# Local transformer: ScalarE writes the masks into PSUM and copies both halves of the turned probabilities

## The reference

```python
q, k, v = heads(shift(x) @ Wqkv)        # 16 heads of 64
q, k = l2norm(q) * q_scale, l2norm(k) * k_scale
q, k = rotate(q, scale), rotate(k, 1 / scale)
# windows of 32 queries; keys of the same window and the one before
sim = einsum('bhwie,bhwje->bhwij', q, look_back(k)) * 8
mask = (i < j) | (i > j + 32) | (j == -1)
attn = softmax(where(mask, -max, sim))
x = einsum('bhwij,bhwje->bhwie', attn, look_back(v)) @ Wo + x
x = (a * gelu(gate)) @ W2 + b2 + x      # a, gate = layernorm(shift(x)) @ W1 + b1
```

## Time and profile before

| | |
|---|---|
| median of the runs | 2441.62 us |
| the profiled execution | 2439.11 us, span 2437.3 us |
| TensorE matmul busy | 2257.1 us (93%) |
| TensorE weight load busy | 1530.4 us (63%) |
| VectorE busy | 1855.8 us (76%) |
| ScalarE busy | 1298.4 us (53%) |
| GpSimd busy | 1154.0 us (47%) |

### The profile page before, as it was taken

One profiled execution on the slowest core, in us unless ns is written; L12 is line 12 of the kernel. 1 busy time (PEld: TensorE's weight loads), 2 busy tenths in 40 slices (PEclk: granted clock), 3 DMA queues, 4 the chain that ended last, 5 costly groups with the idle time before them and its releaser, 6 DMA issues.

```text
span 2437.3 us, 83769 instructions
## 1 busy us (share of the span) xinstructions
PE 2257.1 (93%) x36453; PEld 1530.4 (63%) x36453; DVE 1855.8 (76%) x4174; ACT 1298.4 (53%) x2414; POOL 1154.0 (47%) x855
## 2 busy tenths in 40 slices
PE   8999899889999999999999999999999999979985
PEld 4567554446667666666667676666766676655564
DVE  5742588779988889798888889897888888756612
ACT  3524154355666666656566666656566666525332
POOL 1037300046666556565656556565656556410064
PEclk8989899899999999999999999999999999999898
DMA  9012200000111211121101211021111111130012
GB/s 297 31 31 41 59 1 1 5 27 20 41 29 37 68 33 31 35 68 37 42 20 37 69 45 33 20 68 37 42 26 31 33 46 33 34 109 2 21 37 77
DMA packets 63736, 106.92 MB, mean 44 GB/s; under 512 B 11700, under 2 KB 48831, under 8 KB 56844
## 3 DMA queue, kind: packets, MB, share of 16 engines
q1 hardware_dynamic: 57626, 93.00, 13.5%
q0 software_dynamic: 4736, 8.29, 1.7%
q10 hardware_dynamic: 1010, 0.29, 0.1%
HBM read 42.55 MB, written 13.24 MB: 23 GB/s over the span
## 4 chain that ended last, share of the span: by engine, by line
PE 62%; POOL 12%; DVE 11%; issue 10%; ACT 3%; DMA 2%; SPq 0%; POOLq 0%; ACTq 0%; DVEq 0%
PE ps L2213 10%; PE ps L2316 6%; PE ps L2295 5%; POOL mem L3007 5%; PE ps L2257 4%; PE ps L2234 4%; PE ps L2222 4%; PE ps L2272 3%; POOL mem L3020 3%; PE ps L2382 3%; PE ps L2368 2%; PE ps L2359 2%; PE ps L1196 2%; POOL mem L3014 2%; PE ps L1682 2%
## 5 line engine op out<-in xcount | busy, mean ns | idle before, releaser
L3007 POOL TENSOR_TENSOR mem<-mem 128x512 f32<-128x512 f32 x384 | 571.6, 1495 | 557.2 <-DVE mem L2524 554.0
L2213 PE MATMUL ps<-mem 128*128 128x512 f32 x768 | 380.8, 608 | 8.6 <-ACT mem L2811 3.4
L2839 ACT ACTIVATE mem<-ps 128x512 f32<-128x512 f32 x384 | 221.5, 603 | 155.7 <-PE ps L2234 155.1
L2818 ACT ACTIVATE mem<-ps 128x512 f32<-128x512 f32 x384 | 220.6, 597 | 144.1 <-PE ps L2213 107.3
L2519 DVE TENSOR_TENSOR mem<-ps,mem 128x512 f32<-128x512 f32 x384 | 258.5, 673 | 13.0 <-ACT mem L2818 13.0
L2524 DVE TENSOR_TENSOR mem<-ps,mem 128x512 f32<-128x512 f32 x384 | 261.2, 680 | 0.0
L2234 PEld LDWEIGHTS ps<-mem 128*128 128x128 f32 x1536 | 183.2, 142 | 114.9 <-issue 96.2
L2295 PEld LDWEIGHTS ps<-mem 64*64 64x64 f32 x12288 | 191.7, 135 | 79.7 <-issue 77.5
L2531 DVE TENSOR_REDUCE mem<-mem 128x16 f32<-128x1024 f32 x192 | 232.0, 1208 | 0.0
L3020 POOL TENSOR_TENSOR mem<-mem 128x1024 f32<-128x1024 f32 x95 | 180.7, 1902 | 82.0 <-DVE mem L2592 82.0
L2234 PE MATMUL ps<-mem 128*128 128x128 f32 x1536 | 212.0, 274 | 5.9 <-DVE mem L2564 3.1
(11 more groups left out here) (313 smaller groups left out, 4154.6 us busy)
## 6 DMA issues: line engine op xcount, KB each, us to landing
mem<-mem SPq DMA_DIRECT2D x48, 768.0 KB, 5.8
mem<-in_Wqkv SPq DMA_DIRECT2D x6, 1536.0 KB, 6.7
mem<-mem SPq DMA_DIRECT2D x36, 256.0 KB, 3.5
y<-mem SPq DMA_DIRECT2D x8, 512.0 KB, 6.2
mem<-in_W12T SPq DMA_DIRECT2D x8, 512.0 KB, 7.7
mem<-y SPq DMA_DIRECT2D x16, 256.0 KB, 4.9
mem<-in_L3W SPq DMA_DIRECT2D x16, 256.0 KB, 5.6
mem<-in_L2Wo SPq DMA_DIRECT2D x6, 512.0 KB, 7.0
```

The costliest lines, as they stand in the source:

```text
L2213: e.matmul(self.K.ps[:, o, :], self.columns(u, bb), self.K.l2[l % 2]["Wqkv"][:, 512 * i:512 * i + 512], start=True, stop=True, skip_group_ ...
L3007: e.tensor_tensor(t1[:, cols], t1[:, cols], self.T2[:, cols], ALU.add).then_inc(s("rotated"), 1)
```

## The change

The mask matmuls of `pe_scores` go. In their place ScalarE copies the mask from SBUF (bf16) into the bank (f32) in `a_mask`, one call for each bank and pass, and raises `seeds`; `pe_scores` waits for both of them. `a_mask` has its own waits for the banks. The feature transposes now clear a bank's flags only with the first of four, so that scores add onto what ScalarE wrote into bank 3. `a_turned_p` copies bank 4 behind bank 6 on ScalarE and `v_turned_p` returns at once, in all passes but the last three. In the convolution stage an event with the name `seeds` replaces `bias_parts`, without any other effect.

In an even pass the calls of `a_mask` for the next pass stand behind the second feature copy, in an odd pass behind the last copy of values; in both, ahead of the last two feature copies.

```diff
@@ -2231,7 +2231,8 @@
         after(e, self.freed[o])
         for c in range(4):
             h = 128 * (4 * j + c)
-            last = e.transpose(ps[:, o, 128 * c:128 * c + 128], self.T1[r % 2][k][:, h:h + 128], self.K.ident)
+            last = e.matmul(ps[:, o, 128 * c:128 * c + 128], self.T1[r % 2][k][:, h:h + 128], self.K.ident, start=c == 0,
+                            stop=True, is_transpose=True, skip_group_check=True)
         last.then_inc(s("by_feature"), 1)
         self.freed[o] = [s.at("placed", 4 * r + i + 1)]
 
@@ -2243,11 +2244,8 @@
         e.wait_ge(*s.at("placed", 8 * u + 8))
         if g % 2:
             e.wait_ge(*s.at("padded", u + 1))
-        mask = self.K.maskb[:, 1 if u % 4 == 0 and g % 2 else 0, :]
         banks = self.SCORES
-        for odd in range(2):
-            after(e, self.freed[banks[odd]])
-            e.matmul(ps[:, banks[odd], :], self.K.identb, mask, start=True, stop=False, skip_group_check=True)
+        e.wait_ge(*s.at("seeds", 2 * g + 2))
         for c2 in range(4):
             for wi, wn in enumerate(self.windows(g)):
                 for odd in range(2):
@@ -2597,8 +2595,14 @@
             e.tensor_tensor(p, p, bc(self.sms[r], 2, 64), ALU.mult).then_inc(s("soft"), 1)
         self.fill()
 
+    def scalar_copies(self, g):
+
+        return g + 3 < self.NG
+
     def v_turned_p(self, e, g):
         s = self.s
+        if self.scalar_copies(g):
+            return
         e.wait_ge(*s.at("p_turned", 2 * g + 2))
         if g >= 1:
             e.wait_ge(*s.at("weighed", 2 * g))
@@ -2687,8 +2691,10 @@
             self.a_values(e, 0, n)
         self.a_by_feature(e, 1, 0)
         self.a_by_feature(e, 1, 1)
+        self.a_mask(e, 0, 0)
         self.a_rotate(e, 2, 2)
         self.a_rotate(e, 2, 3)
+        self.a_mask(e, 0, 1)
         self.a_by_feature(e, 1, 2)
         self.a_by_feature(e, 1, 3)
         for g in range(self.NG + 1):
@@ -2723,6 +2729,8 @@
                 if placed:
                     self.a_by_feature(e, g + 2, 1)
                 if this:
+                    self.a_mask(e, g + 1, 1)
+                    self.a_mask(e, g + 1, 0)
                     self.a_beside(e, hl, w, 3)
                 if placed:
                     self.a_by_feature(e, g + 2, 2)
@@ -2763,6 +2771,9 @@
                 if more:
                     self.a_values(e, u + 1, 3)
                 if placed:
+                    self.a_mask(e, g + 1, 0)
+                    self.a_mask(e, g + 1, 1)
+                if placed:
                     self.a_by_feature(e, g + 2, 2)
                 if this:
                     self.a_beside(e, hl, w, 3)
@@ -2859,6 +2870,20 @@
         e.wait_ge(a.sem, a.n)
         e.activation(K.rs[:, c], K.rs[:, c], ACT.Exp, scale=-0.5).then_inc(s("mlp_guessed"), 1)
 
+    def a_mask(self, e, g, odd):
+
+        K, s = self.K, self.s
+        if odd == 0:
+            if g + 1 < self.NG:
+                e.wait_ge(*s.at("placed", 4 * (g + 1) + 2))
+            else:
+                e.wait_ge(*s.at("lessened", 2 * g - 1))
+        elif g + 2 < self.NG:
+            e.wait_ge(*s.at("rotated_half", 4 * (g + 2) + 3))
+        else:
+            e.wait_ge(*s.at("lessened", 2 * g))
+        e.activation(K.ps[:, self.SCORES[odd], :], K.maskb[:, 1 if g % 8 == 1 else 0, :], ACT.Copy).then_inc(s("seeds"), 1)
+
     def a_exp(self, e, g):
         p = view(self.PB[g % 2], "p o c w j -> p (o c w j)")
         e.wait_ge(*self.s.at("lessened", 2 * g + 2))
@@ -2870,6 +2895,10 @@
             e.wait_ge(*s.at("weighed", 2 * g))
         e.wait_ge(*s.at("p_turned", 2 * g + 1))
         e.activation(view(self.PT[:, 0], "p c b h q -> p (c b h q)"), ps[:, self.TURN_P[0], :], ACT.Copy).then_inc(s("p_cols"), 1)
+        if self.scalar_copies(g):
+            e.wait_ge(*s.at("p_turned", 2 * g + 2))
+            e.activation(view(self.PT[:, 1], "p c b h q -> p (c b h q)"), ps[:, self.TURN_P[1], :], ACT.Copy
+                         ).then_inc(s("p_cols_too"), 1)
 
     def a_weighed(self, e, g):
         s, (u, half) = self.s, divmod(g, 2)
```

More of the change, by code:

```diff
@@ L1467 @@
     LEAD = 3
-    TOTALS = dict(weight_sums=2, weight_totals=1, first_weights=1, second_weights=1, tap_rows=32, taps=3, bias_parts=1,
+    TOTALS = dict(weight_sums=2, weight_totals=1, first_weights=1, second_weights=1, tap_rows=32, taps=3, seeds=1,
                   normed=NT, ready_rows=NT, rows_turned=B, cols=B, up=NT, hidden_rows=NT, rounded=NT, rounded_turn=NT, cols2=NT,
@@ L1532, in v_steps @@
         e.wait_ge(v.sem, t)
-        e.tensor_copy(self.parts.bitcast(BF16)[three, 0:512], rest[three]).then_inc(s("bias_parts"), 1)
+        e.tensor_copy(self.parts.bitcast(BF16)[three, 0:512], rest[three]).then_inc(s("seeds"), 1)
         yield
@@ L1645, in tensor @@
         e.wait_ge(*s.at("taps", 3))
-        e.wait_ge(*s.at("bias_parts", 1))
+        e.wait_ge(*s.at("seeds", 1))
         for i in range(self.LEAD):
@@ L1975 @@
                   p_cols=NG, p_cols_too=NG, values_mm=4 * NU, values=4 * NU, values_shifted=16 * (2 * NU - NF),
-                  weighed=2 * NG, out_cols=2 * NG, projected=NU, attention_added=NU, shift_mm=NF, mlp_shifted=NF,
+                  seeds=2 * NG, weighed=2 * NG, out_cols=2 * NG, projected=NU, attention_added=NU, shift_mm=NF, mlp_shifted=NF,
                   mlp_kept=NF, mlp_rows=8 * NF, mlp_turned=2 * NF, mlp_cols=2 * NF, mlp_gated=6 * NF, mlp_up=6 * NF,
```

## The result

The changed kernel takes 2441.05 us (median; 2434.66 to 2454.97) beside 2433.09 us (2421.69 to 2445.67) of the kernel before in the same rounds: a ratio of 1.0036, interval 1.0021 to 1.0051. It is 0.36% slower, some 9 us, where I had forecast 27 us less. The 2441.62 us that the forecast started from was the median of three runs and lies 8.5 us above the median of the same kernel here, so the ratio says more than the two times of 2441 us. The profiled execution took 2444.1 us (span 2442.2), beside 2439.1 (span 2437.3) before.

The account below looks back on a forecast made before the run. TensorE's queue was taken to set the pace nearly everywhere, VectorE's chain in some odd passes (w is g mod 8). Gains of 31.5 - 1.0 - 1.3 - 2 = 27 us from 2441.6 gave 2414.5 us, range 2397 to 2434.

Parts of the forecast that it names:

- the sum of the passes: Eight passes of a half layer: 0.6 + 0.8 + 0.5 + 0.7 = 2.6 us saved; twelve half layers, 31.5 us.
- last passes: Before the last scores: masks stand behind two copies of weighed values on ScalarE, costing 1.3 us.
- up to the first scores: At the start: the second mask waits for VectorE's half rotation and two copies follow, costing 1.0 us.
- TensorE loses the masks: All 96 passes: scores could start where the first mask started, 0.53 us a pass, 51 us in all.
- VectorE's copy: Odd passes: 0.60 us off VectorE's chain where TensorE waits for it, w=1 to 2 and w=7 to 0.
- a sign that I would be wrong altogether: Sign against the forecast: the weighing waits for the second copy, or VectorE waits for ScalarE's guess.
- half arrives: Rival: longer hops through ScalarE or slower masks cost 0.15 us in 96 passes, 14 us less gain, 2428; 17%.
- Stalls, taken as +2: Score bursts: 11 stalls, taken as instruction supply, may lengthen, multiply or drop; -3 to +9 us, taken as +2.
- ScalarE's prices: ScalarE's queue: a mask takes 0.60 us, a copy 585 ns, each 0.49 start to start; 140 us more work.
- Slower: Rival: ScalarE's queue holds the guess behind a waiting mask; +23 us (2464) in 24 passes, +45 in 48; 9%.
- its ring: ScalarE's second mask awaits VectorE's half rotation; VectorE's next unit awaits the guess behind that mask; 0.94 us a pass.
- No difference: Rival: VectorE's odd copies give up to 29 us, but ScalarE's tails take 0.5 in every pass; 2441; 7%.

Follow-up runs that it names:

- e1: Kernel before with only the 93 copies moved to ScalarE, masks left on TensorE; ratio 0.9944 against the kernel before.
- e2: Kernel before with only the masks moved to ScalarE, VectorE keeping its copies; ratio 1.0090 against the kernel before.
- e6: Changed kernel with the masks of w=1, w=2 and the last pass back on TensorE; ratio 0.9967 against the kernel before.
- e7: Changed kernel run once more, unchanged, for a second trace; ratio 1.0027 against the kernel before.
- e3: Changed kernel with the masks of the last pass (g=95) alone back on TensorE; ratio 0.9994 against the kernel before.
- e8: Changed kernel with 128 more TensorE instructions in the warm-up ahead of the first scores; ratio 1.0063 against the kernel before.
- c1: Kernel before run once more, unchanged, for a second trace; ratio 0.9992 against the kernel before.
- e5: Changed kernel with masks on ScalarE only in w=4 and w=5, TensorE laying the others; ratio 0.9941 against the kernel before.
- e4: e3 plus six warming matmuls, results unused, ahead of the turn in w=2; ratio 1.0032 against the kernel before.
- e9: e4 with 128 more TensorE instructions in the warm-up ahead of the first scores; ratio 1.0065 against the kernel before.

## Why the prediction was wrong, step by step

The step that failed is the sum of the passes: 2.6 us a half layer were forecast and 1.2 measured, and the low clock at w=2, which isn't in the sum at all, took it back together with longer waits for instructions. In the profiled executions the time went -27 us by the forecast and +11.6 us as measured (means of two traces each; the ratio of the runs says +9):

| | forecast | measured |
|---|---|---|
| passes without stalls and low clock | -31.5 | -11.8 |
| stalls and low clock in the passes | +2 | +11.6 |
| last passes | +1.3 | +5.8 |
| up to the first scores | +1.0 | +6.0 |

**TensorE loses the masks: 0.53 us a pass.** The step was mis-sized. In w=4 and w=5, where nothing else is in the way, it is 0.44. The first scores stand right behind the last transposes,

```profile
1276.70 1.04 PE L2270 MATMUL ps<-mem 128*128 128x128 f32 x8
1277.67 1.48 PE L2255 MATMUL ps<-mem 64*32 64x64 f32 x128
```

0.97 us start to start. The same two in the kernel before:

```profile
1275.20 1.04 PE L2272 MATMUL ps<-mem 128*128 128x128 f32 x8
...
1276.60 1.48 PE L2257 MATMUL ps<-mem 64*32 64x64 f32 x128
```

1.40, of which 0.53 is the masks: scores start 0.10 us later behind a transpose than a mask does. I had put the scores where the first mask began. Over 96 passes it is 9 us of the ceiling of 51, but only some 2 us of the forecast, in which few passes had the full 0.53.

**VectorE's copy: 0.60 us in the chain of w=1 and of w=7.** Right for w=7 to 0 (0.59 in e1), wrong for w=1 to 2 (0.16). I took VectorE's chain as nearly gapless and so 0.60 shorter. It became shorter up to the next thing that it needs: VectorE's waits for ScalarE's guess of the MLP's norm are 1.2 us (5 of them) before, 6.2 (11, 0.56 each) in e1 and 5.1 (11) in the change. That wait took the place of the copy. Its other waits for ScalarE's guess grew too, from 15.2 us before to 20.1, and by the masks: they are 15.2 in e1 and 20.5 in e2. I had named such waits as a sign that I would be wrong altogether.

**The sum of a half layer: 2.6 us.** By the medians w=7 and w=7 to 0 together gave 0.30 (0.7 forecast): the copy gives 0.59, and the masks take half of it back, as the scores wait for the feature copies pushed behind them:

```profile
1341.01 1.09 ACT L2850 ACTIVATE mem<-ps 128x512 f32<-128x512 f32 x2
...
1340.52 1.09 PE L2270 MATMUL ps<-mem 128*128 128x128 f32 x8 [0.30 <-POOL mem L3049]
1342.16 1.48 PE L2255 MATMUL ps<-mem 64*32 64x64 f32 x128 [0.54 <-ACT mem L2850]
```

w=1 and w=2 together gave 0.2 (0.6). w=3 and w=4 gave 0.43 (0.8), all of it in w=4: in w=3 the masks stand behind the GELU and TensorE waits 0.3 to 0.4 us for them (e6's row 1255.12), where I had the scores start 0.25 us earlier than before. w=5 and w=6 gave 0.37 (0.5). I had worked from the starts in ScalarE's queue, and each of these tails let TensorE go 0.1 to 0.4 us later than I had it. Together 1.3 us a half layer by the medians and 1.2 by the minima, 11.8 us in the ten in the middle. The first half layer, which has no MLP beside it, and the last one up to g=94 gained nothing (116.7 us before and 116.6 after, 101.8 both, by the shorter of two traces); I had counted all twelve alike. (Twelve times 2.6 is also 31.2, not 31.5.) By size this is the largest error, and it is the rival "half arrives" more than the forecast, though not by its mechanism: a mask took no longer than I had it.

**The missing term: TensorE's clock at w=2.** I counted the masks as pure cost. From w=1 to 2 TensorE idles 1.10, 1.59 and 0.32 us in the last seven before the scores (1.11 and 1.60 before), and the masks were work among these holes. Without them the granted clock falls to half in some half layers. Spells that begin between 1.2 us before and 0.5 behind the first scores of w=2 stand in 25 of 55 half layers in the five traces without masks or other work there (3, 6, 6, 6 and 4 of eleven in the change, e7, e2, e3 and e8), and in none of 77 in the other seven (before, c1, e1, e5 and e6 with the masks, e4 and e9 with the six matmuls). Where no stall falls in the same pass, such a spell costs 0.6 to 1.0 us. The time of w=2 to 3 above 16.43 us, summed over ten half layers, is 4.5, 4.0 and 3.1 us where the masks are on TensorE (before, c1, e1), and 12.4, 10.1, 12.0 and 10.8 where they aren't (the change, e7, e2, e3): about 7 us more. e6 puts the masks back and has 3.2; e4 and e9 put other work there and have 6.0 and 5.4. Some 3 of the 7 us are more waits for instructions in this pass (6.9 and 4.2 us in the two traces of the change, 2.9 in each before), and some 4 are the clock. That the missing work brings the spells at the first scores is shown; the two spells of the first trace that stand behind stalls may have come from these, and that part isn't separated.

**Stalls, taken as +2.** In the stretch the scores' waits for "issue" are 9.0 us [10.0 before, rows 2] in one trace of the change and 14.2 in the other, against 3.6 in c1. Those at w=2 last 1.0 to 1.8 us, where they lasted 0.7 to 1.3. In the mean of two traces each that is 5 of the 11.6 us; the range of -3 to +9 held. I had taken them for the supply of instructions, and the packets on q8 show that they are. The other half of the step, that the shifted order in memory decides, is shown by e8: 0.36% for 128 instructions.

**The last passes, +1.3 us.** The late masks are right (1.30 us). I had not seen what this meets: the burst then runs during the load of the next layer's weights and stops for 4.5 to 4.8 us, and the projection behind it runs at the low clock, which had come before the stop, 5.6 to 6.5 us instead of 3.84. e3 takes the masks away and the stop goes; e8 keeps them and the stop goes too: it hangs on the place in the program. But it is not the whole: from the scores of g=94 to the end these two still take 318.7 and 318.4 us, with smaller stalls ahead and a projection of 4.3 to 5.0 us, where e6 takes 310.9, e9 311.8 and e4 313.8. I can place the 1.30 us of the late masks and the stops of single traces, but what fixes this stretch's length over programs stays open.

**Up to the first scores, +6 us in the traces.** Only 0.7 of it is the step that I had put at 1.0: from the first rotation of the transformer to its first scores it takes 38.2 and 38.4 us before, 39.0 and 38.9 after. The other 5.3 us lie ahead of the transformer, where no instruction's work is changed, and go with TensorE's clock: the first rotation starts at 499.7, 503.7, 508.0 and 514.7 us in c1, e7, the kernel before and the change, behind 61, 72, 82 and 96 us at half clock. One program differs by 8 to 11 us in this between two of its executions. So of the +11.6 us of the traces some 5 are such chance, as far as two traces each can tell; what sets the clock there stays open.

**ScalarE's prices were right.** A mask takes 601 ns (0.60 taken). By the Trainium skill (VectorE: DVE Perf Modes, section on the TRN2 errata) I had estimated it 43 ns above a copy from PSUM; the rows above show 12 to 18. By another page of the Trainium skill (ScalarE: Activation LUTs, the tip on placement in the step-by-step section) PSUM is the faster destination; no run here has a copy from SBUF to SBUF at this width, so that isn't tested. The weighing never waited for the second copy.

**The rivals.** "Slower" had the sign right, at 9%, but not the reason: its ring was to cost 0.94 us a pass, and by the minima no pass grew by more than 0.06. TensorE's waits for masks are 6.0 us in the stretch, and the longer waits for the guess lie in w=5, where w=5 to 6 grew by 0.05 us. "No difference" was nearest in time, and by luck, as its 2441 us started from the higher median: taking matmuls away did move the starts by 0.44 us where TensorE was the limit (e5), and VectorE's copies gave 0.59 at w=7; it was other things that ate it.

## What to carry to other kernels

A small piece of work that stands just behind an engine's longest wait is worth less than its start-to-start time, and on TensorE it can be worth less than nothing: look at what the granted clock does after the piece is gone, in that pass. Move work by place, not by kind: here, beside the copies, the masks gain in two passes of eight and, taken with the pass behind, give nothing or harm in the others, and the kernel that moves them only in the two, with the copies, is 0.6% faster than before, as the one with the copies alone is. And what an edit of some ten us in 2400 gives is no larger than what the order of the code in memory gives or takes, so undo each half alone before believing either sum.

## What I had not expected of the hardware

- 128 more instructions in a warm-up, with the same passes behind it, cost 0.36% (1.0063 against 1.0027). The stalls with no releaser come from one set of passes in each execution of a program, not all of them each time (four and eleven in two traces of the kernel before), and at others in the shifted one.
- These stalls are waits for instructions: 229 of 230 end 2.2 to 3.0 us after the start of a 16 KB packet on q8.
- A stall of this kind lasts up to 2.3 us in a quiet stretch of the stage and 3.5 to 5.7 us in seven places while weights are loaded (4.79 at 2137.17, 4.61 at 1088.81). The granted clock is at half behind each of the seven. In the last scores of the change it was at half ahead of the stop already:

```profile
2126.00:2143.00 17.00, 9.46 (x183) 7.99 (x176) 4.15 (x6) 4.10 (x6) 4.26 (x2) 0.50 0.54 142
```

  The kernel before has clock 1.00 and about the same DMA share (0.55) in this stretch.
- A copy by ScalarE from SBUF (bf16) into PSUM, 128 by 512, takes 601 ns, and one from PSUM to SBUF 583 to 600: the direction hardly matters.
- Matmuls that accumulate (`start=False`) add onto what ScalarE wrote into the bank, here in both banks of all 96 passes. The change also makes the transposes clear a bank's flags with the first of four alone; no run here leaves that out.
